# Two-part queries and keys, score products in two row halves of the array, and a subtraction spread over three engines

## The reference

```
q = rope(heads(hn @ wq), pos_sel)
kk = rope(heads(hn @ wk), pos_sel)
v = heads(hn @ wv)
sc = jnp.einsum('bhqd,bhkd->bhqk', q, kk) / np.sqrt(hd).astype(np.float32)
sc = sc + m_sel[:, None]
a = jax.nn.softmax(sc, axis=-1)
o = jnp.einsum('bhqk,bhkd->bhqd', a, v).transpose(0, 2, 1, 3).reshape(b, kc, d) @ wo
```

## Time and profile before

| what | us |
|---|---|
| median of 3 executions (479.44 to 481.64) | 479.98 |
| the profiled execution: its own time | 479.28 |
| its span in the trace | 477.5 |
| attention of batch 0, first score product to last values | 67.16 (255.28 to 322.44) |
| feed-forward of batch 0 and parts of batch 1 | 45.34 (322.44 to 367.78) |
| attention of batch 1 | 70.10 (367.78 to 437.88) |
| PE busy over the span | 438.4 |
| DVE busy over the span | 383.8 |
| ACT busy over the span | 241.3 |
| POOL busy over the span | 294.2 |

### The profile page before, as it was taken

How to read it: one execution, slowest core, us unless ns; L and a number is a source line. 1 busy time by engine, 2 the same in 40 slices (tenths; PEclk the granted TensorE clock), 3 DMA queues, 4 the chain that set the end, 5 groups by cost and what they waited for, 6 DMA issues and landing times.

```text
span 477.5 us, 9894 instructions
## 1 busy us (share of the span) xinstructions
PE 438.4 (92%) x3557; PEld 335.4 (70%) x3557; DVE 383.8 (80%) x1173; ACT 241.3 (51%) x431; POOL 294.2 (62%) x295
## 2 busy tenths in 40 slices
PE   8798999999999987999998999997998999998893
PEld 5587888777777743476775777775796777676692
DVE  4878898788998799868989999865966999881773
ACT  3436555565545527024665665655434666564640
POOL 8366667776677742076665998842000999991374
PEclk9999999999999999998999999999999999999998
DMA  7713442234421211046981000000000000000011
GB/s 237 264 45 91 123 140 91 88 92 136 126 89 46 71 62 45 1 129 213 321 263 47 1 3 2 1 3 0 2 1 0 1 4 1 1 2 2 1 40 50
DMA packets 29256, 33.88 MB, mean 71 GB/s; under 512 B 5748, under 2 KB 24856, under 8 KB 29208
## 3 DMA queue, kind: packets, MB, share of 16 engines
q1 hardware_dynamic: 22976, 24.78, 16.0%
q0 software_dynamic: 3520, 8.40, 6.0%
q10 hardware_dynamic: 2712, 0.06, 0.3%
HBM read 19.59 MB, written 13.63 MB: 70 GB/s over the span
## 4 chain that ended last, share of the span: by engine, by line
PE 38%; POOL 16%; DVE 10%; issue 4%; ACT 3%; POOLq 0%; DVEq 0%
POOL arena L672 9%; PE ps L1023 7%; PE ps L1045 4%; PE ps L1006 4%; PE ps L1117 3%; PE ps L1152 3%; PE ps L708 3%; PE ps L970 2%; PE ps L842 2%; POOL arena L519 2%; PE ps L938 2%; PE ps L1123 1%; PE ps L977 1%; POOL w_lo L631 1%; PE ps L1143 1%
## 5 line engine op out<-in xcount | busy, mean ns | idle before, releaser
L672 POOL TENSOR_SCALAR arena<-arena,nmax 128x511 f32<-128x511 f32 x64 | 108.4, 1705 | 46.6 <-DVE nmax L1857 46.3
L1377 ACT ACTIVATE big<-ps 128x512 f32<-128x512 f32 x128 | 76.0, 600 | 57.5 <-PE ps L1023 54.4
L1857 DVE CUSTOM_DVE_ANT_0 arena<-ps,nmask 128x511 f32<-128x511 f32 x128 | 83.6, 681 | 7.8 <-PE ps L1006 5.5
L1023 PE MATMUL ps<-ident,arena 128*128 128x128 f32 x512 | 77.7, 274 | 2.4 <-POOL arena L672 1.6
L1023 PEld LDWEIGHTS ps<-ident,arena 128*128 128x128 f32 x512 | 59.5, 140 | 20.3 <-issue 10.1
L741 PE MATMUL ps<-wgd_hi,x_hi 128*128 128x512 f32 x128 | 51.6, 403 | 0.0
L1006 PE MATMUL ps<-arena 96*128 96x512 bf16 x128 | 48.2, 383 | 3.3 <-DVE nmax L1857 2.1
L743 PE MATMUL ps<-wgd_hi,x_lo 128*128 128x512 f32 x128 | 50.5, 395 | 0.0
L742 PE MATMUL ps<-wgd_lo,x_hi 128*128 128x512 f32 x128 | 50.4, 394 | 0.0
L519 POOL TENSOR_TENSOR arena<-arena 128x512 f32<-128x512 f32 x30 | 38.7, 1291 | 9.6 <-DVE arena L1501 7.9
L533 POOL TENSOR_TENSOR rq<-vq,minus_half 128x4 f32<-128x4 f32 x16 | 16.2, 1010 | 35.3 <-DVE v L1530 35.3
(11 more groups left out here) (266 smaller groups left out, 1013.0 us busy)
## 6 DMA issues: line engine op xcount, KB each, us to landing
arena<-in_L_attn_x SPq DMA_DIRECT2D x16, 512.0 KB, 4.8
out<-ob_sb SPq DMA_DIRECT2D x16, 512.0 KB, 3.1
w_sb<-in_L_ffn_w SPq DMA_DIRECT2D x2, 1024.0 KB, 10.7
mt_scratch<-nmask SPq DMA_DIRECT2D x8, 256.0 KB, 6.3
mt_scratch<-big SPq DMA_DIRECT2D x8, 256.0 KB
big<-in_L_attn_Wg SPq DMA_DIRECT2D x1, 256.0 KB, 4.2
big<-in_L_attn_WD SPq DMA_DIRECT2D x1, 256.0 KB, 5.1
wqk<-in_L_ffn_wq SPq DMA_DIRECT2D x1, 256.0 KB, 8.3
```

The costliest lines, as they stand in the source:

```text
L672: pool.tensor_scalar(sm[n % SM_RING][:, 0:K - 1], sm[n % SM_RING][:, 0:K - 1], nmax[:, c, h:h + 1], None, ALU.subtract).then_inc(below_rea ...
L1023: mm = pe.transpose(ps[:, 2 + u % 2, k * P:(k + 1) * P], sm[n % SM_RING][:, k * P:(k + 1) * P], ident[:, :])
L1377: act.activation(prT[c % 2][:, h, :, :], ps[:, 2 + u % 2, :].rearrange("p (k n) -> p k n", k=C), ACT.Exp, scale=-1.0).then_inc(prT_ready, 1)
L1857: dve.tensor_tensor_reduce(sm[n % SM_RING][:, 0:K - 1], ps[:, S_BANKS[b][u % RING], 0:K - 1], nmask[b][:, c, 0:K - 1], 1.0, 3.4e38, ALU.ad ...
```

## The change

- `SLOTS` becomes 4 and the parts are single precision rounded for the array (fp32r) in place of bf16: a rounded part and the rest, so 64 values for each head. Of the nine DVE instructions of `parts` two subtractions stay; two copies for each chunk (`high`) come to ACT, in front of other work there.
- Two heads share the 128 rows: `turn_split` makes 16 single precision transposes of 128 columns for a chunk, and `qT`, `kT` hold head 2g in rows 0 to 63 and head 2g+1 in rows 64 to 127. The copies out of PSUM are 512 wide.
- `scores` and `turn_scores` take units in pairs: both waits of a pair come first, then two score products of 64 rows, one in each row half of the array; then the eight transposes.
- `below` is dealt out by `BELOW = "DPADPDPA"`: of eight units three go to DVE, three to POOL, two to ACT. ACT does its unit three units before the exponential of that unit (`A_AHEAD` = 3) and leaves the sign turned, so the exponential's scale is 1 for it.

```
-SLOTS = 6
+SLOTS = 4
...
+BELOW = "DPADPDPA"
+A_AHEAD = 3
...
             def turn_split(b, c):
 
                 done = c + b * C
-                pe.wait_ge(e_ready, done + 1)
                 for m in ((1, 0) if done == C - 1 else range(2)):
+                    pe.wait_ge(e_ready, 2 * done + (2 if done == C - 1 else 1 + m))
                     for half in range(2):
                         pe.wait_ge((qT_ready, kT_ready)[m], done * 2)
-                        for h in range(8):
-                            mm = pe.transpose(psb[0:ER, 2 * m + half, h * P:(h + 1) * P],
-                                              e_sb[c % 2][:, m, 8 * half + h, :, :], ident_b[:, :])
+                        for g in range(4):
+                            mm = pe.transpose(ps[:, 2 * m + half, g * P:(g + 1) * P],
+                                              e_rows[c % 2][:, m, 4 * half + g, :], ident[:, :])
                         mm.then_inc(eT_done[2 * m + half], 1)
...
-                    pe.matmul(ps[:, bank, :], qkT[0][:, hg * HG + h:hg * HG + h + 1, c * P:(c + 1) * P],
-                              qkT[1][:, hg * HG + h:hg * HG + h + 1, :], start=True, stop=True).then_inc(s_done, 1)
+                    for v in (u, u + 1):
+                        c, h = units[v]
+                        g, rows = (hg * HG + h) // 2, slice(h % 2 * 64, h % 2 * 64 + 64)
+                        pe.matmul(ps[:, S_BANKS[b][v % RING], :], qT[rows, g, c * P:(c + 1) * P], kT[rows, g, :],
+                                  start=True, stop=True).then_inc(s_done, 1)
...
                     for u in range(UNITS):
-                        if u + AHEAD < UNITS:
-                            scores(hg, u + AHEAD)
-                        elif not hg_is(hg, TURNS - 1):
-                            scores(hg + 1, u + AHEAD - UNITS)
-                        turn_scores(hg, u)
+                        if u % 2 == 0:
+                            if u + AHEAD < UNITS:
+                                scores(hg, u + AHEAD)
+                            elif not hg_is(hg, TURNS - 1):
+                                scores(hg + 1, u + AHEAD - UNITS)
+                            turn_scores(hg, u)
                         late(hg, u)
...
+            def high(b, c):
+                done = c + b * C
+                act.wait_ge(rope_ready[b], c + 1)
+                for m, s in enumerate((slice(0, 4, 2), slice(0, 4, 3))):
+                    if done >= 2:
+                        act.wait_ge(eT_done[2 * m], done - 1)
+                        act.wait_ge(eT_done[2 * m + 1], done - 1)
+                    src = qk[b][:, c:c + 1, m * D:(m + 1) * D].rearrange("p o (h k) -> p h o k", h=H)
+                    act.copy(e_sb[c % 2][:, m, :, s, :].bitcast(F32R), src.broadcast_to((P, H, 2, HD))).then_inc(e_parts, 1)
...
+                def below(hg, u):
+                    c, h = units[u]
+                    n = unit_number(b, hg, u)
+                    act.wait_ge(sm_ready, n + 1)
+                    act.activation(sm[n % SM_RING][:, 0:K - 1], sm[n % SM_RING][:, 0:K - 1], ACT.Identity,
+                                   bias=nmax[:, c, h:h + 1], scale=-1.0).then_inc(below_ready[2], 1)
...
                     for u in range(UNITS):
                         exponentials(hg, u)
+                        v = u + A_AHEAD
+                        if BELOW[v % len(BELOW)] == "A" and (v < UNITS or hg < TURNS - 1):
+                            below(hg + v // UNITS, v % UNITS)
...
+                for m, (hi, lo) in enumerate(((slice(0, 4, 2), slice(1, 4, 2)), (slice(0, 4, 3), slice(1, 3)))):
+                    dve.wait_ge(e_parts, 2 * done + m + 1)
+                    src = qk[b][:, c:c + 1, m * D:(m + 1) * D].rearrange("p o (h k) -> p h o k", h=H)
+                    dve.tensor_tensor(e_sb[c % 2][:, m, :, lo, :], src.broadcast_to((P, H, 2, HD)),
+                                      e_sb[c % 2][:, m, :, hi, :], ALU.subtract).then_inc(e_ready, 1)
...
                         masked(hg, u)
-                        if u % 2:
+                        if u and BELOW[(u - 1) % len(BELOW)] == "D":
                             below(hg, u - 1)
```

More of the change, by code:

```diff
@@ L46 @@
 ABOVE = 14
-SLOTS = 6
-ER = SLOTS * HD
+SLOTS = 4
 HG = 4
@@ L679, in _ @@
                 for hg in range(TURNS):
-                    for u in range(1, UNITS, 2):
-                        below(b, hg, u)
+                    for u in range(UNITS):
+                        if BELOW[u % len(BELOW)] == "P":
+                            below(b, hg, u)
                         if u == 9 and 0 < hg < TURNS - 1:
                             values_of(b, hg + 1)
-                        if b == B - 1 and hg in (1, 2):
+                        if b == B - 1 and u % 2 and hg in (1, 2):
                             split_w2((hg - 1) * FB + u // 2)
@@ L988, in scores @@
                 def scores(hg, u):
[L989 to L999, removed]
@@ new lines, in scores @@
+                    for v in (u, u + 1):
+                        c, h = units[v]
+                        n = unit_number(b, hg, v)
+                        bank = S_BANKS[b][v % RING]
+                        if hg_is(hg, 0):
+                            if v < RING and bank < 2:
+                                pe.wait_ge(qT_ready, (b + 1) * C * 2 - 1 + bank)
+                            elif h == 0:
+                                pe.wait_ge(qT_ready, (b * C + c) * 2 + 1)
+                        if not first(b, hg) or v >= RING:
+                            pe.wait_ge(sm_ready, n - RING + 1)
+                        if hg_is(hg, 0) and bank >= 6:
+                            if b > 0:
+                                pe.wait_ge(x2_ready, (b - 1) * C + C)
+                            else:
+                                pe.wait_ge(nm_ready[0], C)
@@ new lines, in scores @@
+                    for v in (u, u + 1):
+                        c, h = units[v]
+                        g, rows = (hg * HG + h) // 2, slice(h % 2 * 64, h % 2 * 64 + 64)
+                        pe.matmul(ps[:, S_BANKS[b][v % RING], :], qT[rows, g, c * P:(c + 1) * P], kT[rows, g, :],
+                                  start=True, stop=True).then_inc(s_done, 1)
+                def turn_scores(hg, u):
+                    for v in (u, u + 1):
+                        n = unit_number(b, hg, v)
+                        pe.wait_ge(*below_done(n))
+                        if hg_is(hg, 0) and v == 0:
+                            pe.wait_ge(qT_ready, (b + 1) * C * 2)
+                            pe.wait_ge(kT_ready, (b + 1) * C * 2)
+                        if first(b, hg) and v == 0:
+                            pe.wait_ge(zeroed, 3)
+                        if not first(b, hg) or v >= 2:
+                            pe.wait_ge(prT_ready, n - 1)
+                        for k in range(C):
+                            mm = pe.transpose(ps[:, 2 + v % 2, k * P:(k + 1) * P],
+                                              sm[n % SM_RING][:, k * P:(k + 1) * P], ident[:, :])
+                        mm.then_inc(belowT_done, 1)
@@ L1367, in split @@
                     copy_turned(b, c)
+                    if c < 2:
+                        high(b, c + 2)
             def attention(b):
@@ L1394, in turn_body @@
                     for u in range(UNITS):
+                        if BELOW[u % len(BELOW)] == "A" and u < A_AHEAD and hg_is(hg, 0):
+                            below(hg, u)
+                    for u in range(UNITS):
                         exponentials(hg, u)
+                        v = u + A_AHEAD
+                        if BELOW[v % len(BELOW)] == "A" and (v < UNITS or hg < TURNS - 1):
+                            below(hg + v // UNITS, v % UNITS)
                         if u == 2 and not hg_is(hg, 0):
@@ L1427, in _ @@
                 value(0, c - 1)
+            high(0, 0)
             copy_qk(0, C - 1)
             value(0, C - 1)
+            high(0, 1)
             copy_mask_rows(0, range(3))
@@ L1443, in _ @@
             copy_turned(0, 0)
+            high(0, 2)
             copy_qk(1, 2)
@@ L1446, in _ @@
             copy_turned(0, 1)
+            high(0, 3)
             value(1, 3)
@@ L1946, in _ @@
                     angles(1)
+                elif c == 2:
                     parts(0, 0)
```

81 lines of the change are left out of this document (24 added, 57 removed).

## The result

The changed kernel takes 485.9 us (median of 4, 483.73 to 487.4) against 479.78 of the kernel before: a ratio of 1.0116, 95% interval 1.0065 to 1.0167. It is slower; forecast were 473.5 and 464.5 to 482. The profiled execution has a span of 483.1 us where that of before has 477.5, so 5.6 us are to be found.

| stretch, us | before | after | difference | forecast |
|---|---|---|---|---|
| start to first score product | 255.11 | 255.01 | -0.10 | 0 |
| filling of batch 0, to its first values | 7.76 | 9.55 | +1.79 | 0 |
| batch 0, first to last values | 59.57 | 62.29 | +2.72 | -1.0 |
| feed-forward and parts, to batch 1's first score product | 44.24 | 43.43 | -0.81 | -0.76 |
| filling of batch 1 | 8.09 | 9.86 | +1.77 | 0 |

A forecast was written before the change was run, and what follows sets the result against it. PE was taken to set the pace in batch 0, POOL in turns 1 and 2 of batch 1. Batch 0 -1.0, batch 1 -0.8, -2.9 and -0.2, feed-forward -0.76 gave -5.7, predicting 473.5 us, range 464.5 to 482.

The forecast's parts named there:

- The price of changing the shape: PE between score pairs and transposes: 0.10 us a change, bounds 0.065 and 0.15; three new changes a period, 0.30.
- The forecast period of 3.78: Four units of batch 0 on PE: 3.78 us against 3.84; 3.68 at the low price, 3.93 at the high one.
- The pair: Two score products in different row halves overlap on PE: second one 0.025, so a pair streams in 0.26 us.
- The two halves don't overlap: Rival on score pairs: a pair streams 0.47, a period is 4.20, total 484.4 us (481 to 488); chance 0.15.
- the changes of shape cost nothing beyond those there now: Rival on PE between pairs and transposes: period 3.48, total 466 us (464 to 468); chance 0.27.
- the estimate of 1.3 products for a pair: Alternative for score pairs from the Trainium skill: 0.31 us in place of 0.26, total 476 in place of 473.5.
- The sum: Whole kernel: batch 0 -1.0, batch 1 turns 0, -0.8, -2.9, -0.2, feed-forward -0.76; together -5.7 us.
- ACT's queue becomes the wait: Rival in the attentions: ACT's subtraction before an exponential holds transposes; 483 us if half its 0.6 reaches PE; chance 0.06.
- POOL's relief: Batch 1, fewer subtractions on POOL: turn 1 -0.8 us (16.35 to 15.55), turn 2 -2.9 us (19.44 to 16.5).
- the feed-forward: Beside its second product, ACT's copies at half width remove PE's wait ahead of the last chunk: -0.76 us.
- DVE and ACT hide their parts of the dealt-out work: Attentions: DVE's 3.28 a period becomes 3.08, ACT's extra 0.6 fits in its 1.3 of waiting; worth nothing in batch 0.
- The start of the attention: Before batch 0: ACT's added copies against DVE's relief, taken as 0, with 1.2 us either way as bounds.

The follow-up runs named there:

- run 5: Changed kernel with ACT's copy of heads behind the second exponential of a turn in place of the third; 481.5 us, 1.0034 to the kernel before.
- run 1: Changed kernel with score products and transposes issued unit by unit in place of pairs; 521.11 us.
- run 2: Changed kernel with score products on all 128 rows, so no change of shape between them and the transposes; 484.53 us, 1.0097 to the kernel before.
- run 3: Changed kernel without ACT's share of the subtraction, units alternating between DVE and POOL; 485.74 us, 1.0098 to the kernel before.
- run 4: Kernel before with only the subtraction dealt out to DVE, POOL and ACT (3, 3 and 2 of 8 units); 478.49 us, 0.9962.
- run 8: Kernel before with the subtraction dealt out to three engines only in turns 1 and 2 of batch 1; 478.29 us, 0.9952.
- run 11: Changed kernel with score products four at a time, copy of heads one exponential earlier and idle transposes in the fillings; 479.1 us, 0.9976 to the kernel before.
- run 6: Changed kernel with the transposes of units 0 and 1 ahead of the fourth pair at each attention's start; 484.14 us, 1.0085 to the kernel before.
- run 7: Changed kernel with the copy of heads one exponential earlier and the first transposes ahead of the fourth pair; 481.76 us, 1.0045 to the kernel before.
- run 10: Changed kernel with the copy of heads one exponential earlier and 12 and 8 idle transposes in each filling; 480.26 us, 0.9991 to the kernel before.
- run 12: As run 11, but DVE gives one more of eight subtractions to POOL outside turns 1 and 2 of batch 1; 478.89 us, 0.9976 to the kernel before.

## Why the prediction was wrong

**The price of changing the shape** was taken as 0.10 between the bounds 0.065 and 0.15. Measured are 0.19 into the halves and 0.155 out of them. Both are at or above the upper bound, the price around values. In a period stand two changes of each kind, 0.69 against the 0.40 that was counted with the exit from values. The forecast period of 3.78 became 3.93 and not 4.07, since the hold-up of one group of transposes (0.53 for 0.44) and the 0.025 for each second product fell away; that 3.93 is the value given for the high price is chance. The price turns the -1.0 of batch 0 into +1.25, as run 5 shows, which has no stall between turns (60.82 for 59.57): most steps are longer by 0.09. Changing the tiling mode drains TensorE, says the Trainium skill (TensorEngine Tiling (Array Packing), Tiling Modes); runs 1 and 2 agree, with the two prices above.

**The pair** was costed rightly in its other half: the second product was taken at 0.025 and costs nothing that run 1 against the changed kernel can show. "The two halves don't overlap" is refuted, and so are "the changes of shape cost nothing beyond those there now" and the estimate of 1.3 products for a pair (0.42 for one and for two). The measured 485.9 lies in the range of the first of these rivals, 481 to 488, but for other causes than that one.

**The sum multiplied one period by 16** and gave the fillings and the steps across a turn no term. This is the step that cost most, 6.5 us in the two batches. The eight-and-eight order of the transposes had been shown in the change's rows, but not held against ACT's queue: with the copy of heads between two exponentials it costs 3 x 0.49 in each batch (4.85 against 4.36, run 5). The fillings cost 1.79 and 1.77, where the text had nothing. Where the clock stays up the changed kernel's filling of batch 0 is 8.49 (run 5, the same code up to there), so 0.73 of the 1.79 is waiting and 1.06 is the lower clock. The waiting comes of the pairs: the first transposes stand 3.11 us behind the first score product before the change, 4.14 in run 5, and 3.43 in run 1, which goes unit by unit at the same clock. The sum also left out turn 0 of batch 1, where PE sets the pace as in turn 3 and the same 4 x 0.06 should have stood.

**"ACT's queue becomes the wait"** named the right queue and the wrong instruction. Not the subtraction, but the copy of heads stood in the way, and it had been there before; the stall is the same without the subtraction (run 3).

**POOL's relief** was sized at 3.7 us by the time POOL was busy in turns 1 and 2, 16.35 and 19.44. What counts is how late the values come, and that was 2.46 (runs 4 and 8); POOL's 16.35 in turn 1 didn't delay them, since steps there were 3.84 and 4.27 as in batch 0. The two attentions' own windows already bounded it: 70.10 - 67.16 = 2.94. The mechanism was right in turn 2; batch 1's +0.26 is batch 0's +2.72 less the 2.46. In turn 2 POOL was not without a gap, as forecast, but waited 0.46 and 0.18 for DVE.

**Right were** the feed-forward (-0.81 for -0.76; no wait of PE stands ahead of the last split chunk any more), and that DVE and ACT hide their parts of the dealt-out work: in run 4 batch 0 takes 59.57 from first to last values, as before.

**The start of the attention** (255.01 for 255.11) only looks as forecast, since the granted clock of the two executions differs up to there (0.96 and 1.00 from 10 to 50 us, 1.00 and 0.97 from 200 to 250 us). Among executions with the same clock in all stretches the new parts come out earlier: at 254.37 and 254.60 (runs 2 and 11) against 255.11, and at 255.26 to 256.43 (runs 1, 3, 5, 6 and 7) against 256.58 and 256.71 (runs 8 and 4). So the start gained some 0.6 us, inside the bounds of 1.2 that were given for it.

**Together**, in the profiled executions: fillings +3.56, copy of heads +2.94, price of the changes of shape +2.50, POOL's relief -2.46, feed-forward -0.81, start and rest -0.13, which is the 5.6 us.

## What to carry to other kernels

In this kernel row halves give the second product for nothing but charge some 0.17 us for each change to and from the whole array. One pair between transposes lost 0.09 a period against the old products; four products behind one change passed in 0.66 and won 0.09 (3.75), but only in the periods in which DVE had emptied the banks in time, and not over a whole attention. Where an order is changed from one by one to two by two, look at what stands between the two on the queue that feeds them, and count the ends of loops apart from their period. A busy engine's gain is read from how late its consumers are, not from its own busy time.

## What was not expected of the hardware

In the attentions the clock fell only in the fillings, behind PE's waits (run 1's fall lasted on into the steps behind). In the changed kernel PE idled for 1.46 and 1.01 us and then ran at half speed for some 3 us, at a cost of 1.06 us in batch 0 and about as much in batch 1; idle transposes in the gaps held it at 1.00 (run 10). A wait lets the clock gate throttle and the work behind it starts cold, says the Trainium skill (TensorE: Matmul & The Clock Gate, HAM oscillation — how this bites in real kernels). The page's case is longer waits, for DMA; these rows agree, with waits of 1.46 and 1.01 us for DVE. It is no certain thing: run 5, with the same code up to there, stayed at 1.00 in batch 0 and fell to 0.50 in batch 1. Nor is it the pairs' alone: run 4, with the old score products, fell in batch 1 behind waits of 0.50 and 0.61, where the kernel before stayed at 1.00 behind 0.50 and 0.62. What decides in a single execution stays open.

The clock is also lower in some executions long before the attention:

```profile
10.00:50.00 40.00, 35.82 (x167) 29.34 (x166) 30.22 (x80) 18.28 (x32) 20.82 (x39) 0.91 0.43 128
```

in run 10, whose first score product came at 257.39, and

```profile
10.00:50.00 40.00, 35.73 (x181) 29.33 (x180) 32.71 (x93) 19.68 (x34) 21.81 (x39) 1.00 0.48 140
```

in run 12, where it came at 253.14, with the same code up to the attention. That the clock makes the whole difference is not shown. Spans of single executions can't be compared here below some 4 us, while stretches inside them repeat to some 0.05 us where code and clock are the same.
